# Decoder layers on one core: softmax division in feature layout in three attention stages, key shifts of the routed cross attention on ScalarE

## The reference

```python
x = x + attn(layernorm(x))                       # L0: causal self attention
x = x + cross(ctx, ctx, layernorm(x))            # L0: cross attention, 64 keys a batch
x = x + depths(layernorm(x))                     # L0: mixture of depths on top 128 tokens of a batch
x = x + attn(layernorm(x))                       # L1: self attention, q and k rms-normed
x = x + cross(layernorm(x), ctx, ctx, mask)      # L1: cross attention with a mask
x = x + experts(layernorm(x))                    # L1: 8 experts, top 2

# in every attention, per head:
att = softmax(q @ k.T / sqrt(16))
y = att @ v
return y.reshape(b, t, 256) @ w_proj.T
```

## Time and profile before

| | us |
|---|---|
| median of 3 runs | 2571.24 (2565.96 to 2574.76) |
| profiled execution, its own time | 2568.06 |
| its span | 2566.3 |
| self attention 0 | about 0 to 510 |
| routed cross attention | about 510 to 820 |
| mixture of depths | about 820 to 1040 |
| self attention 1 | about 1040 to 1640 |
| masked cross attention | about 1640 to 1900 |
| experts | about 1900 to 2566 |

### The profile page before, as it was taken

One profiled execution on the slowest core, in us unless ns is written; L12 is line 12 of the kernel. 1 busy time (PEld: TensorE's weight loads), 2 busy tenths in 40 slices (PEclk: granted clock), 3 DMA queues, 4 the chain that ended last, 5 costly groups with the idle time before them and its releaser, 6 DMA issues. The chain is left out here.

```text
span 2566.3 us, 45589 instructions
## 1 busy us (share of the span) xinstructions
PE 2330.6 (91%) x14571; PEld 1519.5 (59%) x14585; DVE 1457.3 (57%) x3885; ACT 1140.1 (44%) x2685; POOL 734.6 (29%) x848
## 2 busy tenths in 40 slices
PE   7999999889996799899999999888886799999998
PEld 5455555545555566533443333445556599999997
DVE  4766676446765443577777767354545733444333
ACT  1666656523331562277777776422221033333332
POOL 3111111044421321333333221153311433333333
PEclk9999999999998999999999999999995899999999
DMA  6222222120000310322222121100009122222221
GB/s 156 88 87 90 87 76 88 31 76 5 5 1 1 105 44 1 93 63 72 66 76 68 58 73 53 40 7 9 9 1 362 57 36 33 36 36 36 36 35 22
DMA packets 135325, 148.85 MB, mean 58 GB/s; under 512 B 25286, under 2 KB 119152, under 8 KB 135024
## 3 DMA queue, kind: packets, MB, share of 16 engines
q1 hardware_dynamic: 119504, 127.23, 16.1%
q0 software_dynamic: 13680, 17.84, 4.3%
q10 hardware_dynamic: 1968, 1.60, 0.4%
...
## 5 line engine op out<-in xcount | busy, mean ns | idle before, releaser
L452 ACT ACTIVATE self_probs<-self_score_ps 128x512 f32<-128x512 f32 (+3 forms) x1024 | 481.0, 516 | 315.0 <-PE self_score_ps L813 162.7
L618 DVE TENSOR_REDUCE self_neg_max<-self_max_ps 128x1 f32<-128x512 f32 x512 | 328.2, 685 | 147.8 <-PE self_max_ps L799 143.3
L799 PE MATMUL self_max_ps<-self_k_stack,self_q_stack 96*128 96x512 bf16 (+3 forms) x1024 | 347.6, 342 | 21.1 <-DVE self_neg_max L615 12.3
L810 PE MATMUL self_score_ps<-self_q_stack,self_k_stack 99*128 99x512 bf16 (+3 forms) x1024 | 342.5, 342 | 1.6 <-ACT self_probs L452 1.6
L2259 ACT ACTIVATE x_stream<-experts_up_ps,experts_bias_now 128x128 f32<-128x128 f32 x568 | 162.4, 369 | 387.7 <-PE experts_up_ps L2480 387.7
L615 DVE CUSTOM_DVE_ANT_0 self_masked<-self_max_ps,self_later 128x128 f32<-128x128 f32 (+3 forms) x512 | 235.4, 488 | 124.1 <-PE self_max_ps L799 112.7
L2480 PEld LDWEIGHTS experts_up_ps<-experts_tileT,x_stream 128*128 128x128 f32 x2272 | 266.7, 193 | 5.3 <-issue 1.8
L2480 PE MATMUL experts_up_ps<-experts_tileT,x_stream 128*128 128x128 f32 x2272 | 267.2, 276 | 1.4 <-DVE x_stream L2396 1.4
L2490 PE MATMUL experts_down_ps<-experts_down,x_stream 128*128 x1136 | 256.8, 379 | 0.0
L824 PE MATMUL self_out_ps<-self_probs,self_values 128*32 128x512 f32 (+3 forms) x2048 | 231.8, 524 | 3.3 <-ACT self_probs L452 1.4
L810 PEld LDWEIGHTS self_score_ps<-self_q_stack,self_k_stack 99*128 99x128 bf16 x1024 | 98.8, 97 | 229.1 <-ACT self_probs L452 171.2
...
## 6 DMA issues: line engine op xcount, KB each, us to landing
...
experts_down<-moe_down_dram SPq DMA_DIRECT2D x8, 1024.0 KB, 10.6
...
```

The costliest lines, as they stand in the source:

```text
L452: act.activation(probs[:, i % 8, 0:w], score_ps[:, (16 * n + i) % 3, 0:w], ACT.Exp).then_inc(exp_done, 1)
L618: dve.tensor_reduce(neg_max[:, n % 2, t, h:h + 1], max_ps[:, i % 2, 0:w], AX, ALU.max, negate=True).then_inc(max_read, 1)
L799: last = pe.matmul(max_ps[:, i % 2, 0:w], q_stack[0:ROWS, h, P * t:P * t + P], k_stack[0:ROWS, h, 0:w], start=True, stop=True)
L810: last = pe.matmul(score_ps[:, m % 3, 0:w], k_stack[0:KROWS, head, P * j:P * j + P], q_stack[0:KROWS, head, S - w:S], start=True, stop=not ...
```

## The change

In both self attentions and the routed cross attention the division keeps features on partitions. ACT copies `out_ps` to `o_raw` as before. SP stores `o_raw` to a DRAM scratch (`out_store`), and loads it back per half batch (`out_load`) in two DMAs: `o_now`, the values only, 16 rows a head, and `sums`, each head's row of sums repeated over 16 rows. ACT replaces the sums by their inverse with a logarithm and an exponential of the negative (`inverted`), and DVE makes one multiplication of 128x512 (`normalise`). In the self attentions its result is `oT`; in the cross attention it stays in `o_now`, which the output product reads. `turn_out`, the reciprocals, `turn_back` and ACT's `turned_back` go, but for the last two groups of a self attention, which keep them (`divide`).

In self attention 1 alone (`MT_STEP`), `turn_maxima` stands behind quarter j=1 instead of j=0, and `copy_shift` one quarter later too.

In the routed cross attention the shifts are copied by ACT (`shift(b, 1)` behind `exponentials(b, 0)`, `shift(b+1, 0)` behind `copy_out(b, 0)`) and no more by POOL. The function is now apart from the masked one, whose work is unchanged. The loads of the depths' weights move from SP's start of batch 2 to behind `out_load(1, 0)`.

```diff
         r_sums = sb("r_sums", [P, TT, GH])
-        o_tok = sb("o_tok", [P, TT, D])
+        o_tok = sb("o_tok", [P, TT, P])
...
-            if j == 0 and n + 1 < N:
+            if j == MT_STEP and n + 1 < N:
                 work.append(("mt", n + 1))
-            if j == 1 and n >= 1:
+            if j == 1 and n == N - 1:
...
-                work += {(1, 1): [("ob", b - 1, 1)], (2, 0): [("e", b - 1, 0)], (2, 1): [("e", b - 1, 1)]}.get((g, j), [])
...
-            if (g, j) == (3, 1):
-                work.append(("ob", b, 0))
...
+                def out_store(n):
+                    b, g = n // NG, n % NG
+                    sp.wait_ge(o_copied, n + 1)
+
+                    wait(sp, out_loaded[g // 2], 32 * b)
+                    sp.dma_start(out_scratch[g // 2, GH * (g % 2):GH * (g % 2) + GH].rearrange("h c d t -> (h c d) t"),
+                                 o_raw[:, n % 2]).then_inc(out_stored[n % 2], 16)
+
+                def out_load(b, half):
+                    for i in range(2):
+                        sp.wait_ge(out_stored[i], 16 * (2 * b + half) + 16)
+
+                    wait(sp, o_done, 2 * (b - 1) + half + 1 if b else 0)
+                    sp.dma_start(o_now[:, half], out_scratch[half, :, 0]).then_inc(out_loaded[half], 16)
+                    sp.dma_start(sums[:, half], out_scratch[half, :, 1, 0:1].to_broadcast([2 * GH, HD, S])).then_inc(out_loaded[half], 16)
...
+                    if b >= 1:
+                        out_store(4 * b - 1)
                     place_shift(4 * b + 1)
+                    if b >= 1:
+                        out_load(b - 1, 1)
...
+                    out_store(4 * b)
...
+                    out_store(4 * b + 1)
...
+                    out_load(b, 0)
...
+                        out_store(4 * b + 2)
                         place_shift(4 * b + 4)
...
-                    wait(act, ot_full, n - 1)
+                    wait(act, out_stored[n % 2], 16 * (n // 2))
                     act.activation(o_raw[:, n % 2], out_ps[:], ACT.Copy).then_inc(o_copied, 1)
 
-                def turned_back(b, k):
-                    act.wait_ge(ob_full, 2 * b + k + 1)
-                    wait(act, e_full, 2 * b)
-                    act.activation(oT[:, k], general[:, bank("ob", b, k)], ACT.Copy).then_inc(ob_copied, 1)
+                def inverted(b, half):
+                    act.wait_ge(out_loaded[half], 32 * b + 32)
+                    act.activation(sums[:, half], sums[:, half], ACT.Ln).then_inc(sums_logged, 1)
+                    act.wait_ge(sums_logged, 2 * b + half + 1)
+                    act.activation(sums[:, half], sums[:, half], ACT.Exp, scale=-1.0).then_inc(sums_inverted, 1)
...
-                        if j == 1 and n + 1 < N:
+                        if j == MT_STEP + 1 and n + 1 < N:
...
+                            inverted(b - 1, 1)
...
+                        if (g, j) == (3, 0):
+                            inverted(b, 0)
...
+                def normalise(b, half):
+                    dve.wait_ge(sums_inverted, 2 * b + half + 1)
+
+                    wait(dve, e_full, 2 * b)
+                    dve.tensor_tensor(oT[:, half], o_now[:, half], sums[:, half], ALU.mult).then_inc(o_done, 1)
...
-                            normalise(n - 1)
+                        if (g, j) == (3, 2):
+                            normalise(b, 0)
+                        if j == 2 and n == N - 1:
+                            divide(n - 1)
...
+                        if (g, j) == (1, 3) and b >= 1:
+                            normalise(b - 1, 1)
...
+            steps = [("S", b, 0)]
+            steps += [("M", b + 1, 0)] * more + [("xt", b + 2, 0)] * next2
+            steps += [("PV", b - 1, 1)] * last + [("xt", b + 2, 1)] * next2
+            steps += [("S", b, 1)]
+            steps += [("M", b + 1, 1)] * more + [("sr", b - 2, 0)] * choice
+            steps += [("q", b + 2, 0)] * next2
+            steps += [("S", b, 2)]
...
+                def out_store(b, half):
+                    sp.wait_ge(o_copied, 2 * b + half + 1)
+
+                    wait(sp, out_loaded[half], 32 * b)
+                    sp.dma_start(out_scratch[half].rearrange("(r i) c d t -> (i c d) r t", r=2),
+                                 o_raw[:, 2 * half:2 * half + 2]).then_inc(out_stored[half], 16)
+
+                def out_load(b, half):
+                    sp.wait_ge(out_stored[half], 16 * b + 16)
+
+                    wait(sp, e_full, 2 * b)
+                    sp.dma_start(o_now[:, half], out_scratch[half, :, 0]).then_inc(out_loaded[half], 16)
+                    sp.dma_start(sums[:, half], out_scratch[half, :, 1, 0:1].to_broadcast([8, HD, S])).then_inc(out_loaded[half], 16)
...
+                for b in range(B):
+                    if b >= 1:
+                        out_store(b - 1, 1)
+                        out_load(b - 1, 1)
+                    out_store(b, 0)
+                    out_load(b, 0)
...
+                    if b == 1:
...
+                for b in range(B):
+                    if b >= 2:
+                        add_normed(b - 2)
+                    if b + 2 < B:
+                        add_bias(b + 2)
...
+                def shift(b, half):
+
+                    act.wait_ge(max_read, 4 * b + 2 * half + 2)
+
+                    wait(act, score_full, SETS * (b - 1) + 2 * half + 2 if b else 0)
+                    least = neg_max[:, b % 2, :, 8 * half:8 * half + 8].unsqueeze(3).to_broadcast([P, TT, 8, S2])
+                    act.activation(shifts[:, half], least, ACT.Copy).then_inc(shifted, 1)
...
+                def inverted(b, half):
+                    act.wait_ge(out_loaded[half], 32 * b + 32)
+                    act.activation(sums[:, half], sums[:, half], ACT.Ln).then_inc(sums_logged, 1)
+                    act.wait_ge(sums_logged, 2 * b + half + 1)
+                    act.activation(sums[:, half], sums[:, half], ACT.Exp, scale=-1.0).then_inc(sums_inverted, 1)
...
+                for b in range(B):
+                    next2 = b + 2 < B
+                    exponentials(b, 0)
+                    shift(b, 1)
+                    if b >= 1:
+                        inverted(b - 1, 0)
...
+                    if b >= 1:
+                        inverted(b - 1, 1)
+                    copy_out(b, 0)
+                    if b + 1 < B:
+                        shift(b + 1, 0)
...
+                def normalise(b, half):
+                    dve.wait_ge(sums_inverted, 2 * b + half + 1)
+                    dve.tensor_tensor(o_now[:, half], o_now[:, half], sums[:, half], ALU.mult).then_inc(o_done, 1)
```

692 lines of the change are left out of this document (507 added, 185 removed).

## The result

The changed kernel takes 2550.99 us (median of 4 runs, 2547.63 to 2557.82) against 2571.59 of the kernel before beside it: ratio 0.9929, 95% interval 0.9904 to 0.9954. The gain is about 18 to 21 us, half of the 39 forecast. Its profiled execution took 2557.82 us, the slowest of the four. The same program was run again with the last experiments, on another chip: 2551.17 us against 2577.01 of the kernel before there, 26 us less, ratio 0.9902 (0.9879 to 0.9924); that profiled execution took 2551.18 us.

The account below looks back on a forecast made before the run. PE was taken as the bound, with waits for DVE and POOL. Self attention 0 -3, self attention 1 -26 and routed cross attention -10 made -39, from a median of 2571.24 to 2532 us; range 2508 to 2556.

Parts of the forecast that it names:

- -3 us: Self attention 0: most of PE's 19.8 us of removed blocks returns as waits for DVE's maxima, leaving -3 us.
- three quarters of a group after the load: Self attentions: the stored and reloaded result is asked for this late or later; a group takes 12.7 us in stage 0.
- at nothing: Self attention 1: ACT's later shift copy would be late next, costed at zero, with 1 us a batch as far end.
- the -26 forecast: Self attention 1: -17.4 for blocks, -12.6 for POOL's cutting, +0.7 for the last group, +3 for port meetings: -26 us.
- the blocks' term: Self attention 1: removing the old division's blocks of four 128x128 turns from PE gains 17.4 us.
- Rival (b): Round trip or shift late by 1.5 us in each of 16 batches: +24, total 2556 us; chance 0.12.
- meetings of the new multiplication with POOL's bias: Self attention 1: DVE's multiplication meets POOL's 2.37 us bias addition; 3 us for seven batches, between 0 and 17.
- The third product: Routed cross attention: DVE's third router product ends some 2.05 us later because POOL's `add_bias` starts right behind `add_normed`.
- forecast +6: Routed cross attention: PE's granted clock falls behind longer waits in batches 2 to 5, +6 us together (0 to +12).
- the blocks count: Routed cross attention, batches 1, 6 and 7: removed blocks and half their waits gain 2.6, 4 and 4 us.
- The end hides its DMAs: Routed cross attention's end: DVE's work of batch 6 precedes the last multiplication; the part up to the products is some 10 us.
- the likeliest case: Whole kernel: the forecast case, 2518 to 2548 us, with a chance of 0.62.

Follow-up runs that it names:

- g2: f3, but self attention 1's load is back behind `place_shift`, and `inverted` and `normalise` of the first half batch come a quarter later: 2520.63 us, ratio 0.9805.
- e2: The changed kernel with `out_load(b, 0)` issued ahead of `place_shift(4b+3)` on SP in self attention 1: 2536.22 us, ratio 0.9871.
- e1: The changed kernel with `MT_STEP` 0, so `turn_maxima` and `copy_shift` are at their old quarters in self attention 1: 2564.84 us, ratio 0.998.
- f3: f1 with the depths' weights' loads issued ahead of SP's loop in the routed cross attention: 2523.29 us, ratio 0.9818.
- f1: The changed kernel with e2's edit and, in the routed cross attention, POOL's `add_bias` held until the second maximum of batch b+1: 2525.89 us, ratio 0.9821.
- g1: f3 with the sums loaded ahead of the values under their own semaphore in the routed cross attention: 2520.22 us, ratio 0.9804.

## Why the prediction was right or wrong

**Self attention 0: right.** -3 us were forecast, and the 15 profiles with the new division lie 0.3 to 5.6 us under the one of the kernel before. That DVE sets the pace, that the waits for the maxima grow to about 20 us (20.7), and that SP's new DMAs cost little, all stand in the rows. One batch of eight had a late load: ACT waits 2.72 us at 161.08, and PE 0.97 and 0.56 behind it, where 0.7 us were charged for SP in seven batches together.

**Self attention 1: wrong, and here the forecast failed.** Two sentences failed together: that the result of the round trip is asked for three quarters of a group after the load and later, and that of the step `MT_STEP` only the shift itself would be late next, "at nothing". Each was looked at alone. On SP `out_load(b, 0)` stands behind `place_shift(4b+3)`; moving `copy_shift` one quarter later moved the load as well, and `inverted(b, 0)` at (3, 0) was not moved: ACT asked 4.5 us after the load, not three quarters of a group. The cost is 1.1 to 1.7 us in an ordinary batch (67.2 to 67.8 us against 66.1 in g2) and far more at the end of the stage: in the last two batches ACT's waits of 3.83 and 2.72 us are followed by PE at half clock (granted 0.50 from 1548 to 1552 and from 1606 to 1610; the first matmul behind the second wait takes 0.61 us instead of 0.38):

```profile
1605.15 0.61 PE L853 MATMUL self_score_ps<-self_q_stack,self_k_stack 99*128 99x512 bf16 x1 [3.66 <-ACT self_probs L485]
```
Batches 6 and 7 up to the last copy took 68.2 and 54.0 us against 67.1 and 49.7 before and 62.5 and 48.9 in e2. With the load in time the stage gave -27.0 in e2 (-21 to -27 in the seven profiles with that edit) and -28.9 in g2, against the -26 forecast: the sum of the terms was right, their meeting on SP was missed. Part of the loss is the clock's: the mean granted clock of the stage was 0.977 in both profiles of the changed kernel, 0.994 before, 0.991 in e2 and 0.988 in g2. That the blocks' term is worth little alone (e1) was not foreseen either. Rival (b), a late round trip with 2556, was given 0.12; it has the right mechanism, but in one stage and once a batch.

**The port in self attention 1.** I charged 3 us for meetings of the new multiplication with POOL's bias. It took 1.46 instead of 0.68 us in six batches; g2's batches are 66.1 us all the same, 4.6 less than before where the forecast made it 3.7 less. So the meeting cost PE little; no run shows by itself how much. The Trainium skill, page "SBUF — State Buffer", section "SBUF: two separate sides", speaks of an exclusive lock for a whole instruction. The second and third product (2.58 and 2.55 us beside POOL's 2.47 and 2.52) agree with it. So does the multiplication of 1.46 us, which met two POOL instructions and not one. DVE:

```profile
1321.72 1.46 DVE L660 TENSOR_TENSOR self_oT<-self_o_now,self_sums 128x512 f32<-128x512 f32 x1
```
POOL:

```profile
1321.48 1.16 POOL L355 TENSOR_TENSOR self_parts<-self_rest,self_parts 128x512 bf16<-128x512 f32 x1 [0.73 <-ACT self_parts L461]
1322.60 2.81 POOL L341 TENSOR_TENSOR x_stream<-x_stream,self_bias 128x1024 f32<-128x1024 f32 x1
```
The multiplication began while POOL wrote the parts, which took their usual 1.16 us, and ended 0.54 us after them; the bias behind took 2.81 instead of 2.36 us, 0.45 more. That is DVE held by the first and POOL's second held by DVE. The prediction counted the bias alone and left out the parts ahead of it.

**Routed cross attention: mechanism right, one term wrong.** The third product, 2.05 us late by the forecast, is 2.14 late (2.55 for 0.41); `spread_scores` at 12.4 us after the start of the batch stands at 635.05, 12.48 after 622.57; the new wait for the multiplication was 1.00; the period with a fallen clock was forecast at 31.5 and 1.7 to 3.4 more and is 33.1, 33.7 and 33.9 in batches 3 to 5, and 34.0 to 34.1 in the second profile. Only batch 2 is longer, 35.9 and 35.0, by the weights' loads that f3 moved. From start to start batches 2 to 5 took 136.6 us (137.2 in the second profile) against 129.3: +7.3, forecast +6. The opening with batches 0 and 1 gave 6.2 us in the first profile, with the granted clock of the kernel before (0.94 in the first 80 us), and 10.9 in the second with 1.00; the forecast was 7.6. One step of the sum had no source: 2.3 us for the four blocks behind `spread_scores`, where the prediction's own 0.44 us a block make 1.8. It did no harm: from `spread_scores` to the next batch it is 18.97 us in f1 where no clock fell, 1.0 of it the wait, so 18.0 for the 18.1 forecast. What failed is the end: batches 6 and 7 were to give 8, since "the blocks count". In batches 6 and 7 less work lies between store and use, and the round trip is late there: PE waits 3.15 and 2.64 us for `o_now`, and in the closing ACT waits 2.85 and 4.97 us for the sums and the choice of tokens comes 2.76 us late where it was 0.76:

```profile
740.47 3.29 PE L1904 MATMUL crossx_general<-crossx_wo,crossx_o_now 128*128 128x256 f32 x8 [3.15 <-DVE crossx_o_now L1752]
...
769.74 3.75 PE L1904 MATMUL crossx_general<-crossx_wo,crossx_o_now 128*128 128x256 f32 x8 [2.64 <-DVE crossx_o_now L1752]
...
794.88 0.63 PE L1917 MATMUL crossx_general<-ident,crossx_pick 128*128 128x128 f32 x4 [2.76 <-DVE crossx_pick L1807]
```
From the start of batch 6 to the depths' start it is 103.8 us against 105.9: -2 where -8 was forecast. "The end hides its DMAs" is the sentence that fell. How much of the 6 us each of these waits took isn't shown; g1, which brings the sums earlier, took 100.4 us there.

**The range** held the time (2551 in 2508 to 2556), the likeliest case did not (2518 to 2548), and the gain was half of what was said, 21 us (26 in the second series) and not 39. That the time fell within the range is owed to its upper part, which was there for a late round trip in all stages.
